# Seventeen of the 24 leading score maxima taken inside the projection stage

## What is computed

```python
Q = (x @ Wq).reshape(B, S, NUM_HEADS, 2 * HEAD_DIM).transpose(0, 2, 1, 3)
K = (x @ Wk).reshape(B, S, NUM_HEADS, 2 * HEAD_DIM).transpose(0, 2, 1, 3)
A1 = jnp.einsum('bhqd,bhkd->bhqk', Q1, K1) * scaling
A2 = jnp.einsum('bhqd,bhkd->bhqk', Q2, K2) * scaling
attn = jax.nn.softmax(A1, axis=-1) - lamb * jax.nn.softmax(A2, axis=-1)
out = jnp.einsum('bhqk,bhkd->bhqd', attn, V)
```

## Time and profile before

| | |
|---|---|
| runs of the kernel | 3346.65, 3347.84, 3353.13 us (median 3347.84) |
| profiled execution | 3346.42 us, span 3344.7 us |
| PE busy | 3129.0 us (94%) |
| DVE busy | 2804.0 us (84%) |
| ACT busy | 2527.6 us (76%) |
| POOL busy | 435.7 us (13%) |
| projections | 0 to 163 us |
| maxima ahead of the loop | 163 to 221 us |
| attention loop | 221 to 2601 us |

### The profile page before, as it was taken

The page is one execution under the profiler, slowest core; times in us unless marked ns, Lnnn a source line. Parts: engine busy times, 40 slices in busy tenths (PEclk is TensorE's granted clock), DMA queues, the critical chain, the costliest instruction groups (busy, mean ns, idle before and its releaser), DMA issues. The chain is left out here.

```text
span 3344.7 us, 84095 instructions
## 1 busy us (share of the span) xinstructions
PE 3129.0 (94%) x29395; PEld 1452.8 (43%) x29396; DVE 2804.0 (84%) x3085; ACT 2527.6 (76%) x4667; POOL 435.7 (13%) x621
## 2 busy tenths in 40 slices
PE   8979999999999999999999999999999768999994
PEld 4513333333333333333333333333333647999994
DVE  3399999999999999999999999999999784333334
ACT  3339999998999999999989998999999432333331
POOL 3000000000000000000000000000000433545553
PEclk9969999999999999999999999999999878999997
DMA  6710101021010101101010101101010751222224
GB/s 169 175 20 9 31 21 28 8 43 28 9 27 24 28 9 27 40 13 28 21 31 9 27 21 31 27 21 28 12 27 21 264 207 26 39 35 38 35 39 117
DMA packets 99950, 151.45 MB, mean 45 GB/s; under 512 B 21793, under 2 KB 64665, under 8 KB 97789
## 3 DMA queue, kind: packets, MB, share of 16 engines
q1 hardware_dynamic: 83644, 127.43, 15.2%
q0 software_dynamic: 15904, 18.66, 3.5%
HBM read 85.74 MB, written 60.30 MB: 44 GB/s over the span
## 5 line engine op out<-in xcount | busy, mean ns | idle before, releaser
L636 DVE TENSOR_REDUCE half_max<-scores 128x2 f32<-128x1024 f32 x2096 | 2386.7, 1212 | 51.3 <-PE scores L542 47.0
L610 ACT ACTIVATE probs<-bank 128x512 f32<-128x512 f32 x4104 | 2226.8, 595 | 183.6 <-PE bank L558 115.5
L590 PE MATMUL bank<-probs,V 128*32 128x256 f32 x16384 | 1318.3, 394 | 66.0 <-ACT probs L610 39.4
L542 PE MATMUL scores<-K,Q 48*128 48x512 f16 x4192 | 830.9, 393 | 29.4 <-DVE half_max L636 24.9
L558 PE MATMUL bank<-Q,K 50*128 50x512 f16 x4104 | 792.8, 380 | 0.3 <-ACT probs L610 0.3
L542 PEld LDWEIGHTS scores<-K,Q 48*128 48x128 f16 x4192 | 201.3, 93 | 920.0 <-DVE half_max L636 744.5
L590 PEld LDWEIGHTS bank<-probs,V 128*32 128x32 f32 x16384 | 323.3, 108 | 620.8 <-issue 537.3
L558 PEld LDWEIGHTS bank<-Q,K 50*128 50x128 f16 x4104 | 376.5, 94 | 113.1 <-ACT probs L610 4.4
L512 POOL TENSOR_SCALAR max_parts<-row_max 128x16 f16<-128x16 f32 x65 | 16.4, 253 | 2144.3 <-DVE row_max L642 2144.3
L1431 ACT ACTIVATE h<-u 128x1024 f32<-128x1024 f32 x71 | 75.0, 1056 | 273.3 <-DVE u L1467 273.3
L1395 PE MATMUL pre<-xgT,w 128*128 128x128 f32 x2272 | 270.5, 278 | 4.3 <-ACT xgT L1425 4.3
(11 more groups left out here) (179 smaller groups left out, 1084.0 us busy)
## 6 DMA issues: line engine op xcount, KB each, us to landing
attended<-att SPq DMA_DIRECT2D x64, 256.0 KB, 2.4
W<-in_L_ffn_w_dram SPq DMA_DIRECT2D x16, 1024.0 KB, 7.0
heads<-attended SPq DMA_DIRECT2D x8, 2048.0 KB, 9.3
Q<-q_parts SPq DMA_DIRECT2D x102, 128.0 KB, 5.4
K<-k_parts SPq DMA_DIRECT2D x102, 128.0 KB, 5.8
q_parts<-parts SPq DMA_DIRECT2D x64, 128.0 KB, 2.4
k_parts<-parts SPq DMA_DIRECT2D x64, 128.0 KB, 2.8
xs<-in_L_attn_x_dram SPq DMA_DIRECT2D x8, 512.0 KB, 4.5
```

The lines of the kernel that those rows point to most:

```text
L542: mm = nc.tensor.matmul(scores[:, b, h, :], Q[p][r, c, up, t * P:(t + 1) * P], K[p][r, up, kc * TC:(kc + 1) * TC], start=True, stop=True)
L590: mm = nc.tensor.matmul(banks[att_bank[s // KB]][32 * u:32 * u + 32, q], V[wp][:, wk, u // 2, :], probs[:, 4 * s % RING + u, q], start=(wk ...
L610: nc.scalar.activation(probs[:, i % RING, :], banks[tile_bank[i]][:], ACT.Exp, scale=SCALE).then_inc(exp_done, 1)
L636: nc.vector.tensor_reduce(half_max[lc % 2][:, :, up, t, kc], scores[:, b], AX.X, ALU.max).then_inc(max_done[b], 1)
```

## The change

Seventeen of the 24 steps that ran ahead of the loop (`PRE = KB + 1`) are taken in blocks 4 to 7 of the projections. A step is four quarters there: one score product of 128 by 512 each, into one of two PSUM banks `first`, and one maximum of 512 columns. Quarters 0 to 67 are dealt out from item 5 of block 4: one behind each of the two matmul calls of an item, and one behind each of the four tiles of `times_wv`. PE waits for the whole first group (`group_loaded`, all 12 DMAs) before quarter 0, and before each later one for the maximum two back. DVE takes the first maximum of an item, then the low part of the item before it, then the second maximum. The values share the two banks of the transposed x (`pv` is a view of `pxT`) to free the two banks, so PE also waits for the copy of the x or of the values that lie there. `half_max` lives in the buffers that both stages hold. The attention adds 17 to four semaphores with four more SyncE instructions, takes the maxima of the first chunk at once, and works off steps 17 to 23 before the loop. Semaphores are merged in `stage_project` (`v_set`) and `stage_join` (`consts_set`, `router_copied`).

```diff
+            KC = S // TC
+            half_max = [held.enter_context(nc.sbuf_tensor(f"half_max{i}", [P, 2, 2, TPC, KC], F32)) for i in range(2)]
+            PRE = KB + 1
...
+    FIRST_AT = CH * ITEMS + 5
...
+        first = [ps(f"first_scores{i}", [P, TC], F32) for i in range(2)]
         pj = [ps(f"pj{i}", [P, TC], F32) for i in range(4)]
-        pv = [ps(f"pv{i}", [P, 2, D], F32) for i in range(2)]
+        pv = [s[:].rearrange("p (j d) -> p j d", j=2) for s in pxT]
...
+        item_quarters, value_quarters, t = {}, {}, 0
+        for n in range(CH, NC):
+            for i in range(ITEMS):
+                if n * ITEMS + i >= FIRST_AT:
+                    item_quarters[n, i] = range(min(t, 4 * PRE), min(t + 2, 4 * PRE))
+                    t += 2
+            value_quarters[n] = range(min(t, 4 * PRE), min(t + TPC, 4 * PRE))
+            t += TPC
...
                 if n >= 1:
                     pe.wait_ge(xT_ready, KD * n)
+                    pe.wait_ge(values_ready, TPC * max(n - 1, 1))
...
             def times_wv(n, tiles):
+                if 1 <= n < NC - 1:
+                    pe.wait_ge(xT_ready, KD * (n + 2))
+                elif n == NC - 1:
+                    pe.wait_ge(values_ready, TPC * n)
                 for j in tiles:
-                    if n >= 1 and j % 2 == 0:
-                        pe.wait_ge(values_ready, TPC * (n - 1) + j + 2)
...
+                    for t in value_quarters.get(n, ())[j:j + 1]:
+                        first_scores(t)
+
+            def first_scores(t):
+                if t == 0:
+                    pe.wait_ge(group_loaded, 16 * 2 * len(ROWS))
+                if t >= 2:
+                    pe.wait_ge(first_done, t - 1)
+                lc, h, up, tile, kc = place(t)
+                r = slice(HALF * h, HALF * h + KR)
+                nc.tensor.matmul(first[t % 2][:], Q[0][r, lc, up, tile * P:(tile + 1) * P],
+                                 K[0][r, up, kc * TC:(kc + 1) * TC], start=True, stop=True).then_inc(first_ready, 1)
...
+                    quarters = item_quarters.get((n, i), ())
                     for k in range(KD):
                         mm = nc.tensor.matmul(pj[i % 4][:], wqk[:, k, i // MC, (i % MC) * P:(i % MC + 1) * P],
                                               xT[n % 2][:, k, :], start=(k == 0), stop=(k == KD - 1))
-                    mm.then_inc(proj_ready, 1)
+                        if k == KD - 1:
+                            mm.then_inc(proj_ready, 1)
+                        for t in quarters[k:k + 1]:
+                            first_scores(t)
...
             for n in range(NC):
                 for i in range(ITEMS):
-                    dve.wait_ge(hi_ready, n * ITEMS + i + 1)
-                    nc.vector.tensor_tensor(parts[:, i % 4, 1, :], pj[i % 4][:], parts[:, i % 4, 0, :],
-                                            ALU.subtract).then_inc(lo_ready, 1)
+                    quarters = item_quarters.get((n, i), ())
+                    for t in quarters[0:1]:
+                        first_maximum(t)
+                    if i > 0:
+                        low_part(n, i - 1)
+                    for t in quarters[1:2]:
+                        first_maximum(t)
+                low_part(n, ITEMS - 1)
+                for t in value_quarters.get(n, ()):
+                    first_maximum(t)
...
+            for s in (*scores_ready, *max_done):
+                sp.sem_inc(s, PRE)
...
-            for i in range(AHEAD):
+            for i in range(PRE, AHEAD):
                 for b in range(2):
                     score_pair(i, i // KB, i % KB * 2 + b)
...
-            for i in range(AHEAD):
+            take_maxima(KB, 0)
+            for i in range(PRE, AHEAD):
                 between = None
-                if i == KB:
-                    between = lambda: take_maxima(KB, 0)
-                if i == KB + 1:
+                if i == PRE:
                     between = lambda: turn_maxima(1, 0, 0)
                 maxima(i, i // KB, i % KB, between)
```

More of the change, by code:

```diff
@@ L120, in stage_project @@
     TURN_AT = ITEMS // 2
+    half_max, PRE, KC, KB = (a[n] for n in ("half_max", "PRE", "KC", "KB"))
+    FIRST_AT = CH * ITEMS + 5
     with ExitStack() as ctx:
@@ L142, in stage_project @@
                  "w_peaked", "peaks_turned", "lift_chain", "lift_bits_ready", "lift_spread", "lift_ready",
-                 "ones_set", "v_zeroed", "v_ones_set", "group_loaded")
+                 "ones_set", "v_set", "group_loaded")
         (wqk_loaded, wv_loaded, zeroed, ident_ready, row_set, wqk_ready, x_loaded, x_turned, xT_ready,
          proj_ready, hi_ready, lo_ready, v_ready, values_ready, w_peaked, peaks_turned, lift_chain,
-         lift_bits_ready, lift_spread, lift_ready, ones_set, v_zeroed, v_ones_set, group_loaded) = (sem(n) for n in names)
+         lift_bits_ready, lift_spread, lift_ready, ones_set, v_set, group_loaded) = (sem(n) for n in names)
         parts_stored = [sem(f"parts_stored{i}") for i in range(4)]
@@ L152, in stage_project, with place @@
         NL = 6 + len(lams)
+        first_ready, first_done = sem("first_ready"), sem("first_done")
+        item_quarters, value_quarters, t = {}, {}, 0
[6 more added lines that the diff above has]
+            t += TPC
+        assert t >= 4 * PRE, t
+        def place(t):
+            i, b, h = t // 4, t // 2 % 2, t % 2
+            at_pair = 2 * (i % KB) + b
+            return i // KB, h, at_pair // 16, at_pair // KC % TPC, at_pair % KC
         ROWS = [(h, i) for i in range(len(Q_PARTS)) for h in range(2)]
@@ L246, in _ @@
             for i in range(2):
-                nc.gpsimd.memset(V[i][:], 0.0).then_inc(v_zeroed, 1)
-            pool.wait_ge(v_zeroed, 2)
+                nc.gpsimd.memset(V[i][:], 0.0).then_inc(v_set, 1)
+            pool.wait_ge(v_set, 2)
             for i in range(2):
-                nc.gpsimd.memset(V[i][:, :, :, HD:HD + 1], 1.0).then_inc(v_ones_set, 1)
-            pool.wait_ge(v_ones_set, 2)
+                nc.gpsimd.memset(V[i][:, :, :, HD:HD + 1], 1.0).then_inc(v_set, 1)
+            pool.wait_ge(v_set, 4)
             for n in range(1, NC):
@@ L368, in _, with low_part, first_maximum @@
                             lift[:, m:m + 1], None, ALU.mult).then_inc(wqk_ready, 1)
+            def low_part(n, i):
+                dve.wait_ge(hi_ready, n * ITEMS + i + 1)
+                nc.vector.tensor_tensor(parts[:, i % 4, 1, :], pj[i % 4][:], parts[:, i % 4, 0, :],
+                                        ALU.subtract).then_inc(lo_ready, 1)
+            def first_maximum(t):
+                dve.wait_ge(first_ready, t + 1)
+                lc, h, up, tile, kc = place(t)
+                nc.vector.tensor_reduce(half_max[lc][:, h, up, tile, kc:kc + 1], first[t % 2][:], AX.X, ALU.max
+                                        ).then_inc(first_done, 1)
             for n in range(NC):
                 for i in range(ITEMS):
-                    dve.wait_ge(hi_ready, n * ITEMS + i + 1)
-                    nc.vector.tensor_tensor(parts[:, i % 4, 1, :], pj[i % 4][:], parts[:, i % 4, 0, :],
-                                            ALU.subtract).then_inc(lo_ready, 1)
+                    quarters = item_quarters.get((n, i), ())
[8 more added lines that the diff above has]
+                    first_maximum(t)
 def stage_attend(nc, a):
@@ L387, in stage_attend @@
     RING = 4 * UNITS
-    KC = S // TC
+    half_max, PRE, KC = (a[n] for n in ("half_max", "PRE", "KC"))
+    assert KB <= PRE < AHEAD - 1
     SCALE = HD ** -0.5 * 2.0 ** (-2 * LIFT)
@@ L394, in stage_attend @@
         att = [sb(f"att{i}", [P, TC], F32) for i in range(2)]
-        half_max = [sb(f"half_max{i}", [P, 2, 2, TPC, KC], F32) for i in range(2)]
         row_max = sb("row_max", [P, 16], F32)
@@ L786, in _ @@
         def _(pool):
[L787 to L790, removed]
+            nc.gpsimd.memset(coef[:], 1.0).then_inc(consts_set, 1)
+            nc.gpsimd.memset(minus_half[:], -0.5).then_inc(consts_set, 1)
+            nc.gpsimd.memset(rb_ones[:], 1.0).then_inc(consts_set, 1)
+            pool.wait_ge(consts_set, 3)
             def add_pairs(k):
@@ L932, in _ @@
             pe.wait_ge(rb_ready, 1)
-            pe.wait_ge(ones_set, 1)
+            pe.wait_ge(consts_set, 3)
             nc.tensor.matmul(lgp[:, 0, :], rb_ones[:], rb_diag[:], start=True, stop=True).then_inc(rw_turned, 1)
@@ L941, in _ @@
                     if k == 4:
-                        pe.wait_ge(rw_copied, 1)
-                        pe.wait_ge(rb_copied, 1)
+                        pe.wait_ge(router_copied, 2)
                     turn_xh(k - 4)
@@ L970, in _ @@
             dve.wait_ge(rw_turned, 1)
-            nc.vector.tensor_copy(rw_T[:].rearrange("p k e -> p (k e)"), turn_x[:, 0, 0:KD * E]).then_inc(rw_copied, 1)
-            nc.vector.tensor_copy(rbias[:], lgp[:, 0, :]).then_inc(rb_copied, 1)
```

(4 more changed lines are left out.)

10 lines of the change are left out of this document (5 added, 5 removed).

## The result

Five runs of the changed kernel took 3363.04 to 3366.55 us, median 3364.7; five of the kernel before, the three shown above and two more, 3346.65 to 3353.13, median 3352.46. The ratio is 1.0044, 95% interval 1.0033 to 1.0056: slower by 0.44%. The difference of the medians is 12.2 us. The profiled execution took 3363.04 us with a span of 3361.3.

A forecast was written before the change was run, and what follows sets the result against it. TensorE bounds the projections, VectorE's maxima the stretch from 160 to 220 us. Added 14.4 + 33.9 + 2.5 + 0.2 = 51.0 us, less 38.5 saved: 12.5 us slower, stated as 3360 us, range 3343 to 3367.

The forecast's parts named there:

- pause: Block 4, before quarter 0: PE stands still until all 12 DMAs of the first group land; 14.4 us added, 12.5 to 15.5.
- 66 products: Blocks 4 to 7: each 48-row product drains PE among 128-row matmuls, 0.515 us each; 33.9 us added, 27 to 39.5.
- clock behind the pause: After PE's idle time in block 4: 5 us at half speed, 2.5 us lost, bounds 0 and 5.
- end of the stage: Before the attention's first pair: four more SyncE instructions cost 0.2 us; the last two products lie beside ACT's last copies.
- clock at 42 us: Early projections: a 2.28 us wait at 42.92 was read as followed by matmuls of full speed; no loss charged.
- saved: Maxima ahead of the attention loop: 34 of 48 pairs go at 1.13 us each, plus 0.1; 38.5 us less.
- landing of the twelfth DMA: First group's loads: the twelfth leaves at 105.55 and lands 8.7 us later, at 114.2, which ends PE's standstill.
- A: Rival on the products in the projections: nothing drains, 0.215 us each; 3340.6 us, faster; chance 0.13.
- B: Rival on the wait in block 4: the group lands by 99.8, no pause; 3343.4 us; chance 0.08 with half forms.
- C: Rival in the projections: the clock stays at half behind the pause, costing another 75 us; 3435 us; chance 0.03.
- D: Rival in the attention's start: 34 maxima are saved but the rest waits for something else; price 2 to 6 us.
- store queue behind a late low part: Projections: SP's two stores queue behind a low part up to one step late; ACT has over 10 us; costs nothing.

The follow-up runs named there:

- e1_pause: Kernel before with only one more wait: TensorE waits for the first group of heads in item 5 of block 4; 3366.23 against 3350.0 us, ratio 1.0045.
- e2_products48: Kernel before plus the change's 68 products and maxima on constants, 48 rows each, no pause, results unused; 3387.51 us, ratio 1.0114 to the kernel before.
- e3_products128: Kernel before plus 68 products and maxima on constants, 128 rows each, no pause, results unused; 3366.37 us, ratio 1.0047 to the kernel before.
- e4_pairs: Changed kernel with both halves of a pair side by side and one maximum of 1024 columns, pause kept; 3346.35 us, ratio 0.9989 to the kernel before.
- e8_pairs_landed: Changed kernel with halves paired, 16 steps from item 4 of block 5, none in block 4; 3333.05 us, ratio 0.9951 to the kernel before.
- e7_low_first: Changed kernel with VectorE taking the low part ahead of both maxima, not between them; 3363.41 us, ratio 1.0042 to the kernel before.
- e5_pairs_late: Changed kernel with halves paired, 16 steps meant from item 4 of block 5, but first pair still in block 4; 3344.81 us, ratio 0.9985 to the kernel before.
- e6_pairs_17: Changed kernel with halves paired, 17 steps meant from item 2 of block 5, still paused in block 4; 3341.87 us, ratio 0.998 to the kernel before.

## Why the prediction held, and where it did not

In the profiled pair, up to the start of the loop:

| term | forecast, us | measured, us | from |
|---|---|---|---|
| pause | 14.4 | 13.7 | 115.27 - 101.4, less the 0.1 of before |
| 66 products | 33.9 | 33.9 | pitch of 1.37 against 0.86 |
| clock behind the pause | 2.5 | 2.7 | what is left of 209.76 - 115.27 = 94.5, less 57.9 of old work and 33.9 |
| end of the stage | 0.2 | 1.0 | last values to first pair: 216.13 - 209.76 = 6.4, before 163.15 - 157.80 = 5.35 |
| clock at 42 us | none | 1.6 | 98.82 - 97.20 |
| sum | 51.0 | 53.0 | 216.13 - 163.15; the terms add to 52.9 |
| saved | 38.5 | 38.4 | 52.8 - 14.4 |
| start of the loop | +12.5 | +14.5 | 235.26 - 220.72 |

**The mechanism held.** The pause, the drained products and the saving are each within 0.7 us of their measure, and each price has a run of its own: the pause and its clock 16 us by itself (e1_pause), the products 34.3 us to the loop (e2_products48), the shape as the reason by the 128 rows (e3_products128). That the terms add is shown by e4_pairs (half of the drains, 17 us off) and e8_pairs_landed (no pause).

**The step that failed is the pricing of the clock.** The prediction charged TensorE's clock once, 2.5 us for 5 us at half speed behind the pause, and put it at nothing elsewhere, because "only the first 221 us count" and because one row had kept its speed. The runs show more in three places. Behind the pause PE ran at half for 6.8 us in the changed kernel and 9.4 in e7_low_first, which has the same pause; read directly from the first four calls and products the loss is 3.2 and 4.4 us (the 2.7 of the table is a remainder, and 3.9 for e7_low_first). At 42 us the clock fell and left PE 1.6 us behind, of which the pause took back 0.7: PE came to it later, and the twelfth DMA landed at 115.2, only 1.0 later than the forecast 114.25. And in the loop the clock was at half for the first 9.7 us, where it had been for 4.9 (last section). Up to the loop this makes 3.6 us in the changed kernel (2.7 + 1.6 - 0.7) and 3.9 in e7_low_first, where nothing was lost at 42 us, for the 2.5 forecast.

**The end of the stage was mis-sized too**, 1.0 us for 0.2. The step said that the last two products lie beside ACT's last copies. ACT's last copy waits for the last value tile on PE, and PE reaches that 2 x 0.515 = 1.03 us later. They lie ahead of that copy, not beside it, so 68 products count and not 66. The four SyncE instructions that were priced at 0.2 do not show: the stretch is 5.35 us before, and 6.37 - 1.03 = 5.34 after.

**The level was low, by 4.7 us** (3360 for 3364.7). The 12.5 us were set on the median of three runs, 3347.84, and the median of all 50 of that kernel is 3349.8: 2.0 us. Another 2.0 us are the later start of the loop, 14.5 for 12.5. The last 0.7 is less than what loop and finish scatter. That the two medians of five differ by 12.2 us, so near to 12.5, is luck: the five of the kernel before lie 2.7 us above its 50.

**One reading was off by 0.45 us.** The 8.7 us to the landing of the twelfth DMA count from the start of its issue, 105.10, not from its end: it landed at 113.8 and not at 114.25. In e7_low_first, where PE and SyncE stood within 0.3 us of the times before, it took 9.1 us, and the pause came out at 14.3, near the forecast, all the same.

**The clock at 42 us was read wrongly.** I took from the earlier trace rows that a wait of 2.3 us leaves the clock up. The same wait of 2.2 to 2.3 us stands at the same place in all profiled executions: the clock stayed up in four of eleven and fell to half for 3.4 or 6.8 us in seven. One row was one outcome of two. It is not the change that decides: with the code of before the clock stayed up once and fell once (e1_pause), with that of the changed kernel it fell once and stayed up once (e7_low_first). Where it fell, PE was 1.3 to 2.9 us behind at block 4; where it stayed up, within 0.3 us of 97.20.

**The rivals.** A (no drain) is refuted by e2 against e3, and its own price was right for a product of 128 rows. B (no pause) is refuted by the 13.7 us; e8_pairs_landed has no pause, at half of the drains. C did not come: the clock is back at 1.00 at 122 us and stays there to the end of the projections. D did not come: 38.4 us of 38.5 are saved, and PE goes from the last leading pair (230.53) to the transposed scores (230.92) without a wait. The store queue behind a late low part costs nothing (e7_low_first).

**A version that beats both** is e8_pairs_landed: 3333.05 us, 0.5% faster than before and about 31 us faster than the change. It moves 16 steps and not 17, pairs the halves, and begins where the first group has landed.

## What to carry to other kernels

Before matmuls are slipped into the gaps of another stage, see whether they use the array in the same shape: here a product of 48 rows between matmuls of 128 cost 0.515 us where one of 128 rows cost 0.22, and two halves side by side cost no more than one. Work put on a full engine also inherits the waits of its operands: the first group landed 49 us before its first use in the old order (113.8 against 163.15), and in the new one the same landing stopped the whole queue for 13.7 us. So look up when the operands land before choosing the place.

## What was not expected of the hardware

The attention loop is the same code in all kernels, yet took 2379.2 to 2385.5 us in the eleven profiled executions. Of before, then of the changed kernel (minimum, median and maximum ns, first and last start):

```profile
L590 PE MATMUL bank<-probs,V x16384: 379/403/636, 220.7 to 2600.6; 128*32 128x256 f32 x200
```

```profile
L654 PE MATMUL bank<-probs,V x16384: 378/403/636, 235.3 to 2618.0; 128*32 128x256 f32 x200
```

That is 2379.9 and 2382.7 us, and 2385.5 in e1_pause. The passes differ among themselves by up to 3.7 us in one execution (297.0 to 300.8 in the changed kernel), and at each turn of the loop the granted clock is at half for 3.4 to 10.2 us. These stretches go with the scatter. Added up over the loop, the clock is at half for 39.3 us in the two shortest loops (e5_pairs_late, 2379.2 us, and e2_products48, 2380.4) and for 52.7 and 54.5 in two of the three longest (e1_pause, 2385.5, and e6_pairs_17, 2383.9); over the eleven the correlation is 0.92. The whole times show the same: of the 45 later runs of the kernel before, the fastest (3344.34 us) had a mean clock of 0.967 and the slowest (3355.22) of 0.962, with a correlation of -0.88.

At the seven turns of the loop the clock is at half for 37.5 us in all, in the kernel before as in the changed one. They differ at the loop's start. Before, then changed (the columns are those of the first table):

```profile
222.00:225.00 3.00, 3.00 (x20) 0.54 (x20) 1.87 (x2) 1.31 (x3) 0.00 (x0) 0.50 0.00 0
226.00:229.00 3.00, 3.00 (x36) 0.88 (x32) 2.88 (x3) 2.62 (x5) 0.00 (x0) 1.00 0.00 0
```

```profile
236.00:240.00 4.00, 4.00 (x28) 0.67 (x24) 2.32 (x2) 1.76 (x4) 0.00 (x0) 0.50 0.01 4
240.00:244.00 4.00, 4.00 (x28) 0.67 (x24) 2.49 (x3) 2.21 (x5) 0.00 (x0) 0.50 0.00 0
```

The clock came back 4.9 us into the loop before and 9.7 us into it in the changed kernel. At half speed that is worth up to 2.4 us, an estimate, of the 2.8 by which the loop took longer. Whether it belongs to the change is open: it was 7.7 us in e7_low_first, the other kernel with 68 single products ahead of 14 pairs, and 3.3 to 5.2 us in all the others. What decides how long the clock stays low, here or at a turn, was not tried.
